# Value products of the grouped-query attention: one fp32 term against three one-pass terms

## What is computed

```python
q = (x @ Wq).reshape(B, S, 32, 128).transpose(0, 2, 1, 3)
k = (x @ Wk).reshape(B, S, 8, 128).transpose(0, 2, 1, 3)   # v in the same way
q, k = _apply_rope(q, cos, sin), _apply_rope(k, cos, sin)
k, v = jnp.repeat(k, 4, axis=1), jnp.repeat(v, 4, axis=1)
logits = where(causal, einsum('bhqd,bhkd->bhqk', q, k) * scale, neg)
attn = softmax(logits, axis=-1)
out = einsum('bhqk,bhkd->bqhd', attn, v).reshape(B, S, 32 * 128) @ Wo
```

## Time and profile before

| | |
|---|---|
| median of three runs | 2729.01 us |
| span of the profiled execution, first to last instruction | 2727.7 us |
| the grouped-query stage | about 1850 to 2660 us of the span |
| one key head (first score to first score) | 102.5 us |
| one unit of bodies 1 to 5 | 8.34 us |
| TensorE's mean granted clock over the span | 0.976 of 2.4 GHz |

### The profile page before, as it was taken

One profiled execution on the slowest core, in us unless ns is written; L12 is line 12 of the kernel. 1 busy time (PEld: TensorE's weight loads), 2 busy tenths in 40 slices (PEclk: granted clock), 3 DMA queues, 4 the chain that ended last, 5 costly groups with the idle time before them and its releaser, 6 DMA issues. The chain is left out here.

```text
span 2727.7 us, 38579 instructions
## 1 busy us (share of the span) xinstructions
PE 2571.7 (94%) x12487; PEld 1838.7 (67%) x12487; DVE 1579.8 (58%) x2919; ACT 1129.2 (41%) x1832; POOL 439.7 (16%) x519
## 2 busy tenths in 40 slices
PE   6999999999999999999999759989999999999996
PEld 3666666666666666666666436658778778778774
DVE  5666666666666666666666260137566566566566
ACT  3455555555555555555555230014234234243231
POOL 0101010101010101010100010004343343242320
PEclk8899999999999999999999969989999999999998
DMA  5122121212121212121211240010110110110001
GB/s 190 44 43 49 41 49 41 49 41 49 41 49 41 49 41 49 41 49 41 49 41 41 69 138 0 0 54 24 39 38 0 38 38 0 38 38 0 16 1 51
DMA packets 46693, 116.86 MB, mean 43 GB/s; under 512 B 5313, under 2 KB 22721, under 8 KB 40514
## 3 DMA queue, kind: packets, MB, share of 16 engines
q1 hardware_dynamic: 46658, 116.40, 16.3%
HBM read 71.81 MB, written 10.49 MB: 30 GB/s over the span
## 5 line engine op out<-in xcount | busy, mean ns | idle before, releaser
L407 DVE TENSOR_REDUCE row_max<-ps_max 128x1 f32<-128x512 f32 x1024 | 678.1, 689 | 294.0 <-PE ps_max L472 270.4
L361 ACT ACTIVATE probs<-ps_score 128x1024 f32<-128x1024 f32 x512 | 525.6, 1027 | 123.8 <-PE ps_score L487 92.5
L472 PE MATMUL ps_max<-KX,Q 68*128 68x512 f32 x1024 | 396.3, 418 | 46.0 <-DMA KX<-content_k 41.2
L485 PE MATMUL ps_score<-Q,K 128*128 128x512 f32 x1024 | 409.1, 400 | 0.5 <-ACT probs L361 0.5
L487 PE MATMUL ps_score<-Q,K 97*128 97x512 f32 x1024 | 405.7, 396 | 0.0
L472 PEld LDWEIGHTS ps_max<-KX,Q 68*128 68x128 f32 x1024 | 194.3, 190 | 207.1 <-issue 150.3
L401 DVE TENSOR_TENSOR Q<-ps_x,Q 64x512 fp32r<-64x512 f32 x256 | 176.5, 690 | 240.7 <-ACT Q L356 238.9
L356 ACT ACTIVATE Q<-ps_x 64x512 fp32r<-64x512 f32 x256 | 151.9, 593 | 365.3 <-PE ps_x L457 363.8
L497 PE MATMUL ps_o<-probs,V_slot 128*32 128x512 f32 x2048 | 245.8, 598 | 1.1 <-ACT probs L361 1.1
L485 PEld LDWEIGHTS ps_score<-Q,K 128*128 128x128 f32 x1024 | 194.2, 190 | 54.9 <-ACT probs L361 12.1
L487 PEld LDWEIGHTS ps_score<-Q,K 97*128 97x128 f32 x1024 | 194.8, 190 | 41.0
(11 more groups left out here) (217 smaller groups left out, 3952.8 us busy)
## 6 DMA issues: line engine op xcount, KB each, us to landing
Q<-Q SPq DMA_DIRECT2D x64, 512.0 KB, 4.3
w_raw<-in_w_qrope SPq DMA_DIRECT2D x32, 512.0 KB, 3.7
wq_raw<-in_wq SPq DMA_DIRECT2D x8, 1024.0 KB, 5.6
wo_raw<-in_wo SPq DMA_DIRECT2D x8, 1024.0 KB, 4.9
w_raw<-in_w SPq DMA_DIRECT2D x6, 704.0 KB, 4.1
Q<-content_q SPq DMA_DIRECT2D x64, 64.0 KB
K<-content_k SPq DMA_DIRECT2D x64, 64.0 KB
wkv_raw<-in_wkv SPq DMA_DIRECT2D x8, 512.0 KB, 3.5
```

What stands on the lines that cost most here:

```text
L361: act.activation(probs[:, j, 2 * half:2 * half + 2, :], ps_score[half][:, :, :], ACT.Exp, scale=SCALE).then_inc(exped, 1)
L407: dve.tensor_reduce(row_max[:, t, j:j + 1], ps_max[t % 2][:, :], axis=AXX, op=ALU.max)\
L472: pe.matmul(ps_max[t % 2][:, :], Q2[0:KC0, b, j, t * P:(t + 1) * P], KX[0:KC0, b, j, :], start=True, stop=True).then_inc(max_made, 1)
L485: pe.matmul(ps_score[half][:, k, :], K1[:, b, t * P:(t + 1) * P], Q1[:, b, j, :], start=True, stop=False)
```

## The change

The turned probabilities and the values are each kept as a high part (ACT's copy, now to fp32r) and a low part (a new DVE subtraction that reads PSUM and the high part). `outputs` makes three one-pass terms in place of one fp32 term. The semaphore of the value copies, `v_ready`, becomes `v_high` and `v_low`, and that of the copies of turned probabilities, `t_taken`, becomes `t_high` and `t_low`; PE waits for the low ones before it writes the bank again. ACT's copy of the unturned values goes to a part of `probs` in place of a part of `probsT`.

```diff
-        V = buf("v1", [P, NB, ST, P])
+        V = [buf(f"v_{k}", [P, NB, ST, P], F32R) for k in ("hi", "lo")]
-        probsT = buf("probsT", [P, 3, S])
+        TURNED = [(0, S), (S, S), (2 * S, 2 * P)]
+        probsT = [buf(f"probsT_{k}", [P, 2 * S + 2 * P], F32R) for k in ("hi", "lo")]
+        values_T = probs[:, 1, 0:NB, :]
...
 # ACT, take_turned
-                n = S if k < 2 else 2 * P
-                act.activation(probsT[:, k, 0:n], ps_t[(u + k) % 2][:, 0:n], ACT.Copy).then_inc(t_taken, 1)
+                at, n = TURNED[k]
+                act.activation(probsT[0][:, at:at + n], ps_t[(u + k) % 2][:, 0:n], ACT.Copy).then_inc(t_high, 1)
...
 # DVE
+            def low_values(kv, b):
+                dve.wait_ge(v_high, NB * kv + b + 1)
+                dve.tensor_tensor(V[1][:, b, :, :], ps_t[b][:, :].rearrange("p (t n) -> p t n", t=ST), V[0][:, b, :, :],
+                                  ALU.subtract).then_inc(v_low, 1)
+
+            def low_turned(i, u, k):
+                dve.wait_ge(t_high, 3 * i + k + 1)
+                at, n = TURNED[k]
+                dve.tensor_tensor(probsT[1][:, at:at + n], ps_t[(u + k) % 2][:, 0:n], probsT[0][:, at:at + n],
+                                  ALU.subtract).then_inc(t_low, 1)
...
                 maxima(i)
                 normalise(i, 0)
+                for b in range(NB):
+                    low_values(kv, b)
                 rope(r, ring + ring_query(2), (START + ring_query(2)) % 2, 0, tk, 0)
                 for u in range(1, NU):
                     maxima(i + u)
+                    low_turned(i + u - 1, u - 1, 0)
+                    low_turned(i + u - 1, u - 1, 1)
                     normalise(i + u, u)
+                    low_turned(i + u - 1, u - 1, 2)
                     if u < NU - 2:
                         rope(...)
                         low_o(i + u - 1, u - 1)
                     else:
                         for k in range(2) if not last else ():
                             rope(...)
                         low_o(i + u - 1, u - 1)
+                for k in range(3):
+                    low_turned(i + NU - 1, NU - 1, k)
                 add_out(0)
                 add_out(1)
                 low_o(i + NU - 1, NU - 1)
...
 # PE, turn
                 if k == 2:
-                    pe.wait_ge(t_taken, 3 * i + 1)
+                    pe.wait_ge(t_low, 3 * i + 1)
...
 # PE, outputs
-                for k, piece in enumerate(pieces):
-                    pe.wait_ge(t_taken, 3 * i + k + 1)
-                    for tile, at in piece:
-                        last = pe.matmul(ps_o[:, tile * P:S], V[:, b, tile, :], probsT[:, k, at:at + S - tile * P],
-                                         start=tile == 0, stop=k == 2)
+                for p, vs in ((0, (0, 1)), (1, (0,))):
+                    for k, piece in enumerate(pieces):
+                        pe.wait_ge((t_high, t_low)[p], 3 * i + k + 1)
+                        for v in vs:
+                            for tile, at in piece:
+                                at += TURNED[k][0]
+                                last = pe.matmul(ps_o[:, tile * P:S], V[v][:, b, tile, :],
+                                                 probsT[p][:, at:at + S - tile * P],
+                                                 start=tile == p == v == 0, stop=k == 2 and p == 1)
...
 # PE, body: ahead of turn(0)
-                        pe.wait_ge(v_ready, NB * (kv + 1))
+                        pe.wait_ge(v_low, NB * (kv + 1))
```

More of the change, by code:

```diff
@@ L1043, in gqa_stage @@
         v_turned = sem("v_turned")
-        v_ready = sem("v_ready")
+        v_high = sem("v_high")
+        v_low = sem("v_low")
         summed = sem("summed")
@@ L1053, in gqa_stage @@
         turned = sem("turned")
-        t_taken = sem("t_taken")
+        t_high = sem("t_high")
+        t_low = sem("t_low")
         pv_made = sem("pv_made")
@@ L1193, in values @@
                 act.wait_ge(made, START + PER * kv + b + 1)
-                act.activation(probsT[:, b, :], ps_r[(START + b) % 2][:, :], ACT.Copy).then_inc(v_taken, 1)
+                act.activation(values_T[:, b, :], ps_r[(START + b) % 2][:, :], ACT.Copy).then_inc(v_taken, 1)
             def turned_values(kv, b):
                 act.wait_ge(v_turned, NB * kv + b + 1)
-                act.activation(V[:, b, :, :], ps_t[b][:, :].rearrange("p (t n) -> p t n", t=ST), ACT.Copy)\
-                   .then_inc(v_ready, 1)
+                act.activation(V[0][:, b, :, :], ps_t[b][:, :].rearrange("p (t n) -> p t n", t=ST), ACT.Copy)\
+                   .then_inc(v_high, 1)
             def softmax(i, u):
@@ L1350, in turn_values @@
                 for t in range(ST):
-                    last = pe.transpose(ps_t[b][:, t * P:(t + 1) * P], probsT[:, b, t * P:(t + 1) * P], ident[:, :])
+                    last = pe.transpose(ps_t[b][:, t * P:(t + 1) * P], values_T[:, b, t * P:(t + 1) * P], ident[:, :])
                 last.then_inc(v_turned, 1)
```

## The result

The changed kernel takes 2776.73 us (median of 4 runs, 2773.79 to 2780.36) against 2727.99 us (4 runs) beside it: a ratio of 1.0178 (95% interval 1.0164 to 1.0193), slower by 49 us. The span of its profiled execution is 2772.0 us against 2727.7.

A forecast was written before the change was run, and what follows sets the result against it. PE was taken to set the pace, with DVE's loop between merges just as long, 8.34 us. Span 2727.7 + 35 of waits + 11 of clock = 2774, and 1.3 for the median: 2775 us, range 2752 to 2790 and a little.

The forecast's parts named there:

- PE's gain: In each unit's value product, twelve one-pass instructions save PE 0.26 us; 17 us over 64 units if PE stays the bound.
- The normal body: Bodies 1 to 5: DVE's step stays 8.34 us, no gain or loss; T is the end of a body's last subtraction.
- The second loop in the prediction: Bodies 1 to 5: score start to reciprocal 6.10 us, plus 1.52, 0.42 and 0.3 to the next score, also 8.34 us.
- The start: Start of a key head: the rope queues behind low_values, maxima(1) moves 2171.20 to 2173.3, and score 2 starts 1.5 us late.
- Body 6: Subtraction 2 waits for ACT's copy of turn piece 2, with both ropes behind it; maxima 7 at 2228.1 against 2224.26.
- The merge: After body 7: merge 0 starts 4.7 us late, at 2240.4 instead of 2235.67; PE's wait ahead grows to nearly 6 us.
- The clock: At the first merge of every key head but the last, the clock falls after PE's wait: 7 falls of 1.6 us, +11.
- The last key head: Bodies 6 and 7 there have no ropes or projections and no cover; their exposed subtractions cost 4 us.
- Rival (a): PE stays the bound and the subtractions are hidden: 2712 us, by columns 2695; chance 0.05.
- rival (b): The parts cancel, for example with subtractions of 0.3 us: 2729 us; chance 0.04.
- Rival (c): The waits come but the clock does not fall: 2764 us; chance 0.25.
- rival (e): More clock falls, also at the wait for T in body 1, or steps of 8.5 us: 2785 to 2795 us; chance 0.21.

The follow-up runs named there:

- x1: Changed kernel with PE's twelve one-pass instructions kept and all of DVE's new subtractions left out; 2724.39 us, ratio 0.9979 to the kernel before.
- x2: Changed kernel with DVE's subtractions and their waits kept, but the old fp32 product of eight instructions on the high parts alone; 2786.83 us, ratio 1.0210.
- y2: y1 with the rope's last addition moved to POOL, POOL's split held back in each body, and piece 2's subtraction put ahead of normalise; 2721.91 us, ratio 0.9952.
- x3: Changed kernel with 20 unused products of 512 columns in PE's wait ahead of piece 2 of turn(7); ratio 1.0135 to the kernel before.
- x5: Changed kernel with POOL's split of output weights in body 2 held back until normalise(1) is over; ratio 1.0166 to the kernel before.
- x4a: Changed kernel with DVE's order changed in body 6 alone (rope, subtraction 2, rope); ratio 1.0184 to the kernel before.
- x6: Changed kernel with PE's eight transposes of the values moved into the middle of query(2); ratio 1.0135 to the kernel before.
- x4: Changed kernel with DVE's order of ropes and subtractions changed in bodies 6 and 7, same DVE work; 2741.14 us, ratio 1.0039.
- y1: x4 with the early value transposes of x6 and the held-back POOL split of x5; 2729.75 us, ratio 0.9988 to the kernel before.

## Why the prediction was right

It said 2775 us with waits of +35 and a clock cost of +11; measured was 2776.7. A key head came out 6.6 us longer, and the forecast was 4.45 + 1.6 = 6.05. The terms one by one:

- **PE's gain**, 0.26 us a unit: x1's units of 8.09 us and the 1.89 us of a free product bear it out. By the rows' distances 1.90 was to be expected. By the distance that the Trainium skill gives for back-to-back products ("TensorE: Matmul & The Clock Gate", section "Wait — 56ns, not 53.3ns?") it would have been 1.63 us; the trace decides for the rows.
- **The normal body** (8.34, no change): 8.3 to 8.4 measured, and 8.5 in x2. The two subtractions of 512 took 1.28 us rather than 1.38, so that DVE kept 0.2 us, but the unit did not shorten. The second loop in the prediction, through PE and ACT, is then the tighter one, and x2 bears this out: it makes PE's part behind the wait longer and leaves DVE's work as it is, and the unit grows to 8.5. y2 loosens both loops and reached PE's own 8.09.
- **The start** (1.5 us): maxima(1) came 1.96 us later after maxima(0) (13.43 instead of 11.47; 2.1 forecast), and 1.25 of it reached the reciprocal. Then came 0.75 us that the prediction had not: the scalings held up by POOL. A PE wait in body 1, piece 2 of `turn(0)` behind the first subtraction (0.65 us), was not named either; it is covered by the wait for T, which ends later.
- **Body 6** (subtraction 2 waits for ACT, 2.3 us on top of the late start): 1.89 us of wait, and 12.98 us from reciprocal 6 to 7 instead of 11.09, 1.9 more.
- **The merge** (T of body 7 to merge 0, 7.3 us; idle time of nearly 6 us): 2248.94, the end of subtraction 2, to 2256.24 is 7.3, and the wait is 5.40. Without the clock, merge 0 is 5.1 us late (1.25 + 0.75 + 1.9, and 1.2 from 12.3 in x3 against 11.1), forecast 4.7. The whole key head is 4.7 us longer without the clock (107.25 in x3), forecast 4.45.
- **The clock** (1.6 us in seven key heads): it fell at the first merge of seven key heads and not at the last one, as forecast, and cost 1.9 us each by x3.
- **The last key head** (4 us): 93.6 us from its first reciprocal to the last `add_out` instead of 88.2, 5.3 more. The wait ahead of its merge is 0.66 us and the clock stays up there, but it is at 0.50 in two stretches before it (2670 to 2673 and 2680 to 2683 us among them), behind waits of 2.07 and 1.48 us of PE's transposes for DVE. The prediction had no fall there. In x5, where the clock stays at 1.00 through these bodies and the scalings cost 0.8 us less, the same stretch takes 91.5 us.
- **The sum.** The stage came out about 50 us longer, some 4 more than forecast. The profiled span is only 44 us longer: in that execution the part ahead of the stage was 4 us shorter and the part behind it 1.5 us. The first reciprocal of the stage stands anywhere from 1846.9 (x4a) to 1863.3 us (x6) in kernels that are alike ahead of it, so this is no effect of the change. That the median came within 2 us of 2775 is in part luck.

Both claims on causes are shown: DVE alone brings the loss (x2), and reordering without less work takes most of it away (x4, 1.0178 to 1.0039). Rival (a), that PE stays the bound, falls with the waits of PE on `probsT_lo`, and rival (b), that the parts cancel, with the time. Rival (c), no fall of the clock, is what x3 had to bring about by force. Of rival (e), units of 8.5 us did not come, and the falls beyond the seven are those in the last key head.

## What to carry to other kernels

An engine that is busy for 58% of the span can have next to no room in the loop that matters (here 1.81 us in 8.34): walk one period of each engine's queue and add the new instruction to it. In an in-order queue, ask of each added instruction what stands behind it and who waits for that; here the same 208 added DVE instructions came with 49 us more than before or with 4 us less (y1), by order and timing alone. And where a wait ahead of matmuls is long enough to drop the clock, a gain of under a microsecond elsewhere can vanish into the moment at which the clock comes back; keep PE busy in a test kernel before you call such an edit worthless.

## What was not expected of the hardware

- The four scalings of `normalise`, SBUF to SBUF with one tensor input, took 1.27 to 1.28 us alone and 2.11 us beside POOL's subtraction (x5 takes the overlap away and has the 1.27 back). All of the loss is in the first of them: 1.12 us instead of 0.29, and the second starts at 2192.68, where POOL's subtraction ends by the profile. DVE's subtractions from PSUM, which ran beside POOL's cast and subtraction just before (2190.13 to 2191.41), took 1.28 us, as elsewhere. The Trainium skill ("SBUF — State Buffer", section "SBUF: two separate sides") has DVE in a 2-port mode and GpSimd contend for one port pair as an exclusive lock. The trace agrees: a scaling that came second waited until POOL's instruction was over. That the scalings run in such a mode is shown by no run here; and before the change the two overlapped by 0.1 us (2175.02 to 2175.12) without a loss.
- The cost of one fall of the clock is not a constant: the first merge and its wait were longer by 1.9 us in the changed kernel, by 1.4 to 2.6 in x5 and x6 (13.7 to 14.9 us up to `add_out` against 12.3 with PE busy). It goes with when the clock fell (2.7 us after PE went idle in the changed kernel's rows, 4.5 in x5's) and with how long into the merge 0.50 lasted (3.8 or 5.6 us). In the changed kernel nearly the same cost came back in each key head, merges of 4.4 to 4.7 us; in x6 three values came in turns.
